# Attention of layer 1: the packed products of two steps in one visit to the array, where each step had its own

## The chip, the cores and the metric

One core of a Trainium2 chip runs the whole program. The metric is device time in microseconds (us). All data lie in the device's memory at the start and the results are written back there. The engines that matter here are TensorE (PE in the profile, with its weight loads as PEld), VectorE (DVE), ScalarE (ACT) and GpSimd (POOL); SyncE (SP) issues the DMAs.

## What is computed

The program has two layers on four images of 56x56 pixels and 256 channels. Layer 0 is a windowed attention. Layer 1 is full attention over the 3136 pixels of an image, and then an expert network. The change touches only the full attention of layer 1. Cut to what matters, its reference is:

```python
def _L1_attn_ref(x, w_qkv, b_qkv, w_out, b_out):
    qkv = x @ w_qkv + b_qkv                       # x: (4, 3136, 256), eight heads of 32
    q, k, v = jnp.split(qkv, 3, axis=-1)
    ...
    dots = jnp.einsum('bhid,bhjd->bhij', q, k) * scale
    attn = jax.nn.softmax(dots, axis=-1)
    out = jnp.einsum('bhij,bhjd->bhid', attn, v)
    ...
    return out @ w_out + b_out
```

The kernel subtracts from the dots of a query their exact maximum, takes the exponential, multiplies by V and by ones (the second gives the softmax's denominator), and divides at the end.

## The kernel before

`layer1_attend` works on eight *quads* (`QUADS = 2 * B`): four heads of one image each. A quad is 175 *steps* (`STEPS = NG * KT`): 7 groups `j` of 448 queries times 25 tiles `t` of 128 keys (the last tile of 64). The first quad and the last are written out, the six between are one loop body.

In step `n` TensorE makes four score products, one for each head (L1219, 98 rows by 128 columns of weights, 448 columns streamed), into three PSUM banks that rotate: product `i` waits until ScalarE has taken the exponential of product `i - 3` (L1348, output `a_P`). Between the scores stand the products that find the maxima for the *next* quad (L1150, the same shape, names `a_hk`, `a_hq`): 700 for a quad, spread by `maxima_by` over steps 4 to 167, so that a step has four or five. They too have three banks (`MAXES = 3`): product `i` waits until VectorE has reduced product `i - 3` to its row maximum (L1248, output `a_tops`). Steps 0 to 3 and 168 to 174, and the whole last quad, have none.

After the scores of a step comes a *burst*. Its parts are *packed*: four products with 32 columns of weights each, one for each head, side by side in the array, so that they run at the same time. There are three kinds:

- `mix` (L1170): one step's exponentials times V, into the bank MIX.
- `sum_pair` (L1186): the exponentials of two steps, added up by GpSimd (L1371, output `a_added`), times ones, into the bank SUM.
- for the last tile of a group, which has no partner, the exponentials times ones directly (L1175).

Which parts stand in the burst after step `n` is set by a small planner, `bursts()`. A mix is due after the scores of the next step, a sum three steps after its second step (`SUM_LAG = 3`). ScalarE's order follows from it: `TAKE_AT` and `TAKE_SUMS_AT` say before which step's exponentials ScalarE copies MIX and SUM out (L1318, L1323). The first mix of a group waits for that copy (`taken`).

VectorE goes through the steps in order: a step's maxima, and then, in the 7th to 11th step of a group, one of four reciprocals of the previous group's sums (`invert`, L1271, a quarter each) or the multiplication by them (`divide`, L1277). The exponentials lie in a ring of five steps (`RING = 5`), GpSimd's sums in a ring of three pairs.

Of the kernel before, what the change touches and what calls it, by code (L numbers as in the profile page):

```python
# [854 lines left out]
def layer1_attend(nc, A, S):  # L855
# [5 lines left out]
    with ExitStack() as ctx:  # L861
# [7 lines left out]
        STEPS = NG * KT  # L869
# [74 lines left out]
        def bursts():  # L944

            out, mixes, sums = [], [], []
            for n in range(2 * STEPS):
                j, t = divmod(n % STEPS, KT)
                mixes.append((n // STEPS, n % STEPS))
                if t % 2 == 1:  # L950
                    sums.append((n, (n // STEPS, j, t // 2)))
                parts = []
                if True:
                    while sums and sums[0][0] <= n - SUM_LAG:
                        parts.append(("sum",) + sums.pop(0)[1])
                    while mixes and mixes[0][0] * STEPS + mixes[0][1] < n:
                        parts.append(("mix",) + mixes.pop(0))
                out.append(parts)
            return out[:STEPS], out[STEPS:]

        opening, steady = bursts()
        tail = [part for parts in steady for part in parts if part[1] == 0]
        carried = [[(part[0], part[1] - 1) + part[2:] for part in parts] for parts in steady]
# [1193 lines left out]
```

## Time and profile before

| | us |
|---|---|
| median of 3 runs | 7947.33 (7942.66 to 7951.0) |
| the profiled execution, whole | 7931.02 |
| its span in the trace | 7929.2 |
| full attention of layer 1, from its first product to its last | 1789 to 6679 |
| thereof the first 700 maxima alone | 1789 to 2163 |

Over the span PE is busy 90%, DVE 68%, ACT 51% and POOL 47%. A matmul's busy time includes the time it takes to pass through the array, so neighbours overlap: what the engine spends on one is read from the distance between two starts, not from the durations. The same holds of VectorE's and ScalarE's instructions: a merged row of five says when the first started and when the last ended. Times in the text are from the span's start.

### The profile page before, as it was taken

To read this page: it belongs to the slowest core of one execution; us is meant where nothing else is said; L and a number is where in the kernel's file an instruction comes from. 1 tells how busy PE (TensorE), PEld (TensorE's weight loads), DVE (VectorE), ACT (ScalarE), POOL (GpSimd) and SP (SyncE) were. 2 spreads that over 40 slices of the span, in tenths; PEclk is the share of its full clock that TensorE was granted. 3 is DMA by queue.
4 is the path that set the end of the run, shared out by engine and by line. 5 is a ranking of instruction groups with operands and counts; after the bars stand their busy time and mean duration, and the time that the engine had idled before them with its cause. 6 is when DMAs were issued, how large, how long until landed. Compare 5 with 4: busy or idle time off the path is not lost. (4 is left out here: it accounts for less than half of the span.)

```text
span 7929.2 us, 152182 instructions
## 1 busy us (share of the span) xinstructions
PE 7120.8 (90%) x47408; PEld 4323.5 (55%) x47408; DVE 5376.1 (68%) x12877; ACT 4022.7 (51%) x9367; POOL 3714.0 (47%) x2395
## 2 busy tenths in 40 slices
PE   4459998989999999999999999999999888709999
PEld 2347776655455455455455455455455334608888
DVE  3359997659977677677677677677677102618888
ACT  0049997220055655565565555555565664104444
POOL 4011111110066666666666666666666665365554
PEclk8779999995599999999999999999999999859999
DMA  5442323871001201211211211211211102611221
GB/s 158 137 118 68 98 70 93 253 234 44 13 23 30 64 24 38 58 26 36 57 34 28 60 36 26 57 35 33 59 30 37 28 3 67 205 33 56 62 57 31
DMA packets 403136, 519.85 MB, mean 66 GB/s; under 512 B 64096, under 2 KB 355474, under 8 KB 399063
## 3 DMA queue, kind: packets, MB, share of 16 engines
q1 hardware_dynamic: 379687, 469.02, 21.9%
q0 software_dynamic: 22640, 40.75, 1.9%
q8 instruction: 421, 6.90, 0.4%
q14 instruction: 388, 3.18, 0.1%
HBM read 339.07 MB, written 200.10 MB: 68 GB/s over the span
## 5 line engine op out<-in xcount | busy, mean ns | idle before, releaser
L1248 DVE TENSOR_REDUCE a_tops<-a_ps 128x1 f32<-128x448 f32 (+1 forms) x5600 | 3071.8, 612 | 1092.9 <-PE a_ps L1150 1075.2
L1371 POOL TENSOR_TENSOR a_added<-a_P 128x896 f32<-128x896 f32 x1344 | 2799.3, 2102 | 2095.8 <-ACT a_P L1348 2095.8
L1348 ACT ACTIVATE a_P<-a_ps 128x448 f32<-128x448 f32 (+1 forms) x5600 | 2656.6, 547 | 2123.5 <-PE a_ps L1219 2081.9
L1219 PE MATMUL a_ps<-a_qp,a_kp 98*128 98x448 f32 (+1 forms) x5600 | 2154.1, 400 | 104.2 <-ACT a_P L1348 77.2
L1150 PE MATMUL a_ps<-a_hk,a_hq 96*128 96x448 f32 (+1 forms) x4900 | 1818.4, 381 | 2.0 <-DMA a_hq<-scratch_q 1.9
L1219 PEld LDWEIGHTS a_ps<-a_qp,a_kp 98*128 98x128 f32 (+1 forms) x5600 | 1028.9, 187 | 1296.0 <-ACT a_P L1348 741.0
L1170 PE MATMUL a_ps<-a_P,a_vt 128*32 128x448 f32 (+1 forms) x11200 | 1335.1, 549 | 0.0
L1150 PEld LDWEIGHTS a_ps<-a_hk,a_hq 96*128 96x128 f32 (+1 forms) x4900 | 916.4, 187 | 263.6 <-DVE a_tops L1248 170.3
L1186 PE MATMUL a_ps<-a_added,a_ones 128*32 128x448 f32 x5376 | 649.0, 555 | 0.0
L1170 PEld LDWEIGHTS a_ps<-a_P,a_vt 128*32 128x32 f32 (+1 forms) x11200 | 290.1, 109 | 513.9 <-issue 386.4
L550 ACT ACTIVATE n_P<-n_sm,n_mx 112x280 f32<-112x280 f32 x896 | 467.9, 522 | 108.4 <-DVE n_mx L498 108.3
L1271 DVE RECIPROCAL a_sums<-a_sums 128x112 f32<-128x112 f32 x224 | 185.0, 835 | 488.8 <-ACT a_sums L1323 488.8
L451 PE MATMUL n_ps<-n_idn,n_P 112*98 112x112 f32 x2688 | 421.2, 267 | 10.2 <-DVE n_P L508 10.2
L448 PE MATMUL n_ps<-n_idn 112*112 112x112 f32 x1792 | 373.1, 291 | 30.7 <-ACT n_PTs L557 29.8
L498 DVE CUSTOM_DVE_ANT_0 n_sm<-n_ps,n_bias 112x280 f32<-112x280 f32 x896 | 349.2, 445 | 72.3 <-PE n_ps L440 48.7
L557 ACT ACTIVATE n_PTs<-n_ps 98x336 f32<-98x336 f32 x896 | 391.1, 437 | 2.6 <-PE n_ps L451 2.0
L1138 PE MATMUL a_ps<-a_kp,a_qp 96*128 96x448 f32 (+1 forms) x700 | 370.2, 726 | 22.4 <-DMA a_kp<-scratch_k 22.4
L414 POOL CAST n_qp<-n_qn 128x784 fp32r<-128x784 f32 x32 | 52.5, 1639 | 673.7 <-DMA n_kn<-scratch_qk 338.2
L508 DVE TENSOR_SCALAR n_P<-n_P,n_rc 112x280 f32<-112x280 f32 x896 | 334.2, 415 | 16.0
L1951 ACT ACTIVATE e_h<-e_ps,e_b 128x512 f32<-128x512 f32 (+1 forms) x256 | 172.0, 672 | 336.2 <-PE e_ps L1911 311.8
L1924 PE MATMUL e_ps<-e_w2h,e_hTh 128*128 128x256 f32 (+1 forms) x1024 | 295.4, 289 | 37.0 <-DVE e_widest L2033 37.0
L448 PEld LDWEIGHTS n_ps<-n_idn 112*112 112x112 f32 x1792 | 255.4, 183 | 112.5 <-ACT n_PTs L557 98.9
(195 smaller groups left out, 7787.2 us busy)
## 6 DMA issues: line engine op xcount, KB each, us to landing
a_qp<-scratch_q SPq DMA_DIRECT2D x168, 224.0 KB, 3.9
a_kp<-scratch_k SPq DMA_DIRECT2D x96, 320.0 KB, 5.5
a_hk<-scratch_k SPq DMA_DIRECT2D x84, 336.0 KB, 5.0
scratch_t<-o_ts SPq DMA_DIRECT2D x56, 448.0 KB, 5.5
scratch_vw<-scratch_v SPq DMA_DIRECT2D x56, 392.0 KB
n_vt<-scratch_vw SPq DMA_DIRECT2D x64, 343.0 KB
a_hq<-scratch_q SPq DMA_DIRECT2D x84, 200.0 KB, 3.2
e_w<-in_w SPq DMA_DIRECT2D x16, 1024.0 KB, 7.1
```

The costliest lines, as they stand in the source:

```text
L448: pe.matmul(PS[0:TT, turn_bank(m), 384:384 + TT], idn[:, :], idn[:, :], start=True, stop=True)
L451: last = pe.transpose(PS[0:CHUNK, turn_bank(m), TT * c:TT * c + TT], P[:, m % RP, k0:k0 + CHUNK], idn[:, :])
L550: act.activation(P[:, m % RP, :], sm[:, m % 4, :], ACT.Exp, bias=mx[:, m % 8:m % 8 + 1], scale=-1.0, accum_out=rs[:, m % 8:m % 8 + 1]).the ...
L557: act.activation(PTs[:, m % 8, :], PS[0:CHUNK, turn_bank(m), 0:3 * TT], ACT.Copy).then_inc(copied, 1)
L1138: pe.matmul(PS[0:rows_of(t), i % FIRST_BANKS, 0:GW], qp[0:96, hh, 128 * t:128 * t + rows_of(t)], kp[0:96, hh, GW * k:GW * k + GW], start=T ...
L1150: pe.matmul(PS[0:rows_of(t), MAX + i % MAXES, 0:GW], hq[:, 128 * t:128 * t + rows_of(t)], hk[:, GW * k:GW * k + GW], start=True, stop=True ...
L1170: last = pe.matmul(PS[HD * hh:HD * hh + HD, MIX, 0:GW], vt[0:rows, t, HD * hh:HD * hh + HD], P[0:rows, (2 * n + hh // 2) % (2 * RING), hh ...
L1186: last = pe.matmul(PS[HD * hh:HD * hh + HD, SUM, 0:GW], ones[:, :], added2[:, (2 * (PAIRS * j + u) + hh // 2) % 6, hh % 2, :], start=(u == ...
L1219: pe.matmul(PS[0:rows_of(t), i_s % 3, 0:GW], kp[0:98, hh, 128 * t:128 * t + rows_of(t)], qp[0:98, hh, GW * j:GW * j + GW], start=True, sto ...
L1248: dve.tensor_reduce(tops[0:rows_of(t), KT * hh + t, k:k + 1], PS[0:rows_of(t), bank, 0:GW], AX_X, ALU.max).then_inc(topped, 1)
L1348: act.activation(P[0:rows_of(t), (2 * n + pair) % (2 * RING), hh % 2, :], PS[0:rows_of(t), (4 * n + hh) % 3, 0:GW], ACT.Exp).then_inc(expe ...
L1371: pool.tensor_tensor(added2[:, a % 6, :, :], P[:, (2 * n + pair) % (2 * RING), :, :], P[:, (2 * n + 2 + pair) % (2 * RING), :, :], ALU.add ...
```

## The change

One condition in the planner. Before, each step has its burst; now only the steps of odd number inside a quad have one, and it holds everything that is due by then: two mixes, and a sum for nearly every burst. A quad has 175 steps, so the last burst of a quad is after step 173, the next after step 1 of the following quad, and that one has the mixes of three steps. Sums whose third step is even come one step later than before. `maxima_by`, and so the order of VectorE's work, stays as it was.

```diff
                 if t % 2 == 1:
                     sums.append((n, (n // STEPS, j, t // 2)))
                 parts = []
-                if True:
+                if n % STEPS % 2 == 1:
                     while sums and sums[0][0] <= n - SUM_LAG:
                         parts.append(("sum",) + sums.pop(0)[1])
                     while mixes and mixes[0][0] * STEPS + mixes[0][1] < n:
                         parts.append(("mix",) + mixes.pop(0))
```

The order of TensorE's instructions in the first quad, in steps with maxima. L1219 are scores, L1150 are products for maxima, L1186 is a sum and L1170 a mix. Before:

```order
L1186 MATMUL a_ps<-a_added,a_ones 32x448 x4
L1170 MATMUL a_ps<-a_P,a_vt 32x448 x4
L1219 MATMUL a_ps<-a_qp,a_kp 128x448
L1150 MATMUL a_ps<-a_hk,a_hq 128x448
L1219 MATMUL a_ps<-a_qp,a_kp 128x448
L1150 MATMUL a_ps<-a_hk,a_hq 128x448
L1219 MATMUL a_ps<-a_qp,a_kp 128x448
L1150 MATMUL a_ps<-a_hk,a_hq 128x448
L1219 MATMUL a_ps<-a_qp,a_kp 128x448
L1150 MATMUL a_ps<-a_hk,a_hq 128x448
L1170 MATMUL a_ps<-a_P,a_vt 32x448 x4
```

The same engine and quad now, the end of a stretch of sixteen scores and maxima and the burst behind it:

```order
L1219 MATMUL a_ps<-a_qp,a_kp 128x448
L1150 MATMUL a_ps<-a_hk,a_hq 128x448
L1219 MATMUL a_ps<-a_qp,a_kp 128x448
L1150 MATMUL a_ps<-a_hk,a_hq 128x448
L1219 MATMUL a_ps<-a_qp,a_kp 128x448
L1150 MATMUL a_ps<-a_hk,a_hq 128x448
L1219 MATMUL a_ps<-a_qp,a_kp 128x448
L1150 MATMUL a_ps<-a_hk,a_hq 128x448
L1186 MATMUL a_ps<-a_added,a_ones 32x448 x4
L1170 MATMUL a_ps<-a_P,a_vt 32x448 x8
```

A visit to the array with one or two packed products came after four or five maxima; now one with three comes after eight or nine.

VectorE's order where the reciprocals stand, which is the same before and now. L1248 are maxima, L1271 reciprocals, L1277 the multiplication:

```order
L1248 TENSOR_REDUCE a_tops<-a_ps 128x1 x19
L1271 RECIPROCAL a_sums<-a_sums 128x112
L1248 TENSOR_REDUCE a_tops<-a_ps 128x1 x4
L1271 RECIPROCAL a_sums<-a_sums 128x112
L1248 TENSOR_REDUCE a_tops<-a_ps 128x1
L1248 TENSOR_REDUCE a_tops<-a_ps 64x1
L1248 TENSOR_REDUCE a_tops<-a_ps 128x1 x3
L1271 RECIPROCAL a_sums<-a_sums 128x112
L1248 TENSOR_REDUCE a_tops<-a_ps 128x1 x4
L1271 RECIPROCAL a_sums<-a_sums 128x112
L1248 TENSOR_REDUCE a_tops<-a_ps 128x1 x4
L1277 TENSOR_TENSOR a_yo<-a_y,a_sums 128x448
```

Nothing moved on VectorE; but of the steps whose maxima stand ahead of a reciprocal, those of even number have no burst behind them any more.

TensorE where a group of odd number ends (the second group of the first quad), now; L1175 is the last tile times ones. Before, the two L1170 stood in two bursts, with a step's scores between them:

```order
L1219 MATMUL a_ps<-a_qp,a_kp 128x448
L1150 MATMUL a_ps<-a_hk,a_hq 128x448
L1186 MATMUL a_ps<-a_added,a_ones 32x448 x4
L1170 MATMUL a_ps<-a_P,a_vt 32x448 x4
L1175 MATMUL a_ps<-a_P,a_ones 32x448 x4
L1170 MATMUL a_ps<-a_P,a_vt 32x448 x4
L1219 MATMUL a_ps<-a_qp,a_kp 128x448
```

The last mix of a group and the first of the next, which waits for the copy of the bank between them, now share a burst. The same piece before:

```order
L1170 MATMUL a_ps<-a_P,a_vt 32x448 x4
L1175 MATMUL a_ps<-a_P,a_ones 32x448 x4
L1219 MATMUL a_ps<-a_qp,a_kp 128x448
L1150 MATMUL a_ps<-a_hk,a_hq 128x448
L1219 MATMUL a_ps<-a_qp,a_kp 128x448
L1150 MATMUL a_ps<-a_hk,a_hq 128x448
L1219 MATMUL a_ps<-a_qp,a_kp 128x448
L1150 MATMUL a_ps<-a_hk,a_hq 128x448
L1219 MATMUL a_ps<-a_qp,a_kp 128x448
L1150 MATMUL a_ps<-a_hk,a_hq 128x448
L1186 MATMUL a_ps<-a_added,a_ones 32x448 x4
L1170 MATMUL a_ps<-a_P,a_vt 32x448 x4
```

## Rows read from the trace of the kernel before

**Rows 1.** Stretches: first maxima; quads with maxima; last quad; behind the attention.

```profile
core 0: us, PE busy (x) PEld busy (x) DVE busy (x) ACT busy (x) POOL busy (x), PEclk, DMA share, GB/s
1778.16:2162.90 384.74, 370.21 (x700) 198.34 (x700) 373.05 (x702) 0.00 (x0) 3.62 (x1) 0.50 0.12 26
2164.00:6162.00 3998.00, 3948.99 (x24597) 2071.81 (x24598) 2899.45 (x5175) 2375.43 (x4976) 2439.03 (x1171) 0.99 0.17 40
6162.00:6682.00 520.00, 460.81 (x2935) 171.88 (x2934) 30.18 (x41) 341.98 (x736) 360.31 (x174) 1.00 0.04 11
```

**Rows 2.** Timeline of PE, two steps with four maxima each, and their bursts.

```profile
start us, us, engine line op out<-in xcount [idle before <-releaser]
3003.44 0.96 PE L1170 MATMUL a_ps<-a_P,a_vt 128*32 128x448 f32 x8
3004.33 0.47 PE L1219 MATMUL a_ps<-a_qp,a_kp 98*128 98x448 f32 x1
3004.64 0.37 PE L1150 MATMUL a_ps<-a_hk,a_hq 96*128 96x448 f32 x1
3004.84 0.36 PE L1219 MATMUL a_ps<-a_qp,a_kp 98*128 98x448 f32 x1
...
3005.87 0.37 PE L1150 MATMUL a_ps<-a_hk,a_hq 96*128 96x448 f32 x1
3006.17 0.96 PE L1186 MATMUL a_ps<-a_added,a_ones 128*32 128x448 f32 x8
3006.95 0.94 PE L1170 MATMUL a_ps<-a_P,a_vt 128*32 128x448 f32 x8
3007.82 0.47 PE L1219 MATMUL a_ps<-a_qp,a_kp 98*128 98x448 f32 x1
```

**Rows 3.** Timeline of PE, the next step, with five maxima.

```profile
3008.96 0.37 PE L1219 MATMUL a_ps<-a_qp,a_kp 98*128 98x448 f32 x1
3009.22 0.48 PE L1150 MATMUL a_ps<-a_hk,a_hq 96*128 96x448 f32 x1
3009.53 0.36 PE L1219 MATMUL a_ps<-a_qp,a_kp 98*128 98x448 f32 x1
3009.75 0.47 PE L1150 MATMUL a_ps<-a_hk,a_hq 96*128 96x448 f32 x1
3010.14 0.58 PE L1170 MATMUL a_ps<-a_P,a_vt 128*32 128x448 f32 x4
```

**Rows 4.** Timeline of DVE over the same steps and the next.

```profile
3005.04 2.21 DVE L1248 TENSOR_REDUCE a_tops<-a_ps 128x1 f32<-128x448 f32 x4 [0.52 <-PE a_ps L1150]
3008.54 2.75 DVE L1248 TENSOR_REDUCE a_tops<-a_ps 128x1 f32<-128x448 f32 x5 [0.52 <-PE a_ps L1150]
3011.20 0.84 DVE L1271 RECIPROCAL a_sums<-a_sums 128x112 f32<-128x112 f32 x1
3011.97 2.15 DVE L1248 TENSOR_REDUCE a_tops<-a_ps 128x1 f32<-128x448 f32 x4
```

**Rows 5.** Waits of PEld (its own, and of DVE) from 3000 to 4000 us.

```profile
engine line waited for: us in total, times, longest us
PEld a_ps L1150 <- DVE a_tops L1248: 41.9, 164, 0.4
...
DVE a_tops L1248 <- PE a_ps L1150: 275.2, 257, 31.5
```

**Rows 6.** Line L1138, the first 700 maxima: its starts and waits.

```profile
L1138 PE MATMUL a_ps<-a_kp,a_qp x700: 575/734/742, 1788.9 to 2158.5; 96*128 96x448 f32 x168, 96*64 96x448 f32 x7
its engine sat idle before it (us, times) until:
  DVE a_tops L1248: 169.2, 683
```

**Rows 7.** Timeline of PE, the step in which the reciprocal of rows 4 delays VectorE.

```profile
3011.03 0.47 PE L1219 MATMUL a_ps<-a_qp,a_kp 98*128 98x448 f32 x1
...
3012.59 0.47 PE L1150 MATMUL a_ps<-a_hk,a_hq 96*128 96x448 f32 x1
3012.99 0.96 PE L1186 MATMUL a_ps<-a_added,a_ones 128*32 128x448 f32 x8
```

**Rows 8.** Timeline of all engines, one step of the last quad at a group's end.

```profile
6390.42 0.88 PE L1219 MATMUL a_ps<-a_qp,a_kp 98*128 98x448 f32 x3
6391.01 1.85 ACT L1348 ACTIVATE a_P<-a_ps 128x448 f32<-128x448 f32 x4 [1.35 <-PE a_ps L1219]
6391.61 0.47 PE L1219 MATMUL a_ps<-a_qp,a_kp 98*128 98x448 f32 x1 [0.31 <-ACT a_P L1348]
6392.00 0.96 PE L1170 MATMUL a_ps<-a_P,a_vt 64*32 64x448 f32 x8
6392.78 0.93 PE L1175 MATMUL a_ps<-a_P,a_ones 64*32 64x448 f32 x8
6393.03 0.54 ACT L1318 ACTIVATE a_y<-a_ps 128x448 f32<-128x448 f32 x1 [0.16 <-PE a_ps L1170]
```

**Rows 9.** GpSimd's sums from 3000 to 4000 us.

```profile
L1371 POOL TENSOR_TENSOR a_added<-a_P 128x896 f32<-128x896 f32 x293 | 610.6, 2103 | 389.4 <-ACT a_P L1348 389.4
```

**Rows 10.** Timeline of PE between two quads, at the lower clock: a burst of two.

```profile
4466.84 1.72 PE L1186 MATMUL a_ps<-a_added,a_ones 128*32 128x448 f32 x8
4468.33 1.72 PE L1170 MATMUL a_ps<-a_P,a_vt 128*32 128x448 f32 x8
4469.98 0.87 PE L1219 MATMUL a_ps<-a_qp,a_kp 98*128 98x448 f32 x3
```

## The prediction

> **What bounds the kernel now.** I first cut the span into stretches [rows 1]. The seven quads whose maxima are made beside them take from 2164 to 6162 us, 571 us each, with PE busy 98.8% of the time, DVE 73%, ACT 59%. A busy PE is not yet a bound, so I read its timeline next, by distances between starts. In a step with four maxima [rows 2] the second product starts 0.31 us behind the first (3004.33, 3004.64), the following ones 0.205 apart (3004.64 to 3005.87 are six distances), and the burst 0.30 behind the last (3006.17). Scores and maxima of such a step take 3004.33 to 3006.17, 1.84 us, without a wait. The burst of one mix takes 0.89 (3003.44 to 3004.33), that of sum and mix 1.65 (3006.17 to 3007.82); so a packed product more costs 0.76, and of the 0.89 some 0.14 is the way back to the full array.
>
> The step with five maxima looks different [rows 3]. By distances it would take 1.84 + 0.205 = 2.05; it takes 2.32 (3007.82 to 3010.14). Its last two maxima have a record of 0.48 and 0.47 us in place of 0.37: their weights were loaded late, after a wait. Rows 4 tell for what: VectorE's five reductions take 2.75 us, the last of them 0.61, so they follow each other every (2.75 - 0.61)/4 = 0.53 us, while TensorE offers a maximum every 0.41. With three banks product m+3 waits for reduction m. The view of waits counts 164 such waits in a thousand microseconds, only 42 us in all [rows 5], because four maxima are just what three banks and one reduction absorb, and then the burst gives VectorE time. The first 700 maxima, which have no bursts between them, show the limit naked [rows 6]: 369.6/700 = 0.528 us each, 683 of them waiting for VectorE. So the kernel is bound by TensorE, and VectorE stands right behind it, with the burst of every step as its time to catch up.
>
> **The change, part by part.** Two steps that stood apart now form one phase of eight scores, and behind it one burst of three packed products. Per pair of steps; a quad has 87.5 of them, all eight quads 700.
>
> *Bursts.* Before 0.89 + 1.65 = 2.54, now 1.65 + 0.75 = 2.40: 0.14 less, 700 times: -98 us.
>
> *Phases with maxima.* From the phase's start, the first maximum's product starts at 0.31, its reduction 0.40 later (3004.64 to 3005.04 [rows 2, 4]), at 0.71; reduction m ends at 0.71 + 0.61 + 0.53m. The product that waits for it is recorded 0.06 later (3008.54 + 0.61 = 3009.15 against 3009.22 [rows 3, 4]) and, its weights loaded late, streams another 0.11 later: 1.49 + 0.53m. The burst follows 0.29 behind. For five maxima the last waits for m = 1: 2.02 + 0.29 = 2.31, and the row has 2.32, so the recurrence holds. For eight, m = 4: 3.61 + 0.29 = 3.90, against 2 x 1.84 = 3.68 before, and 3.50 if nobody waited. For nine, 4.43, against 1.84 + 2.32 = 4.16. A quad has its 700 maxima on 82 pairs: 38 with eight and 44 with nine. 38 x 0.22 + 44 x 0.27 = 20.2 us, times seven quads: +141 us.
>
> *Reciprocals.* The one at 3011.20 holds the next reduction up for 0.77 (3011.97) [rows 4]. Before, a burst stands behind each, and hides most of it: the phase behind it takes 1.96 instead of 1.84 (3011.03 to 3012.99) [rows 7], and of the four in a group one or two show at all: some 0.15 us a group. Now two of the four stand between the maxima of an even step and of an odd one, inside a phase in which VectorE already sets the pace, and nothing hides them: 0.76 each. In the four groups of even number the multiplication stands there as well; its own place isn't in these rows, but with its 448 columns it is nearest to a reduction, 0.53. So 14 x 0.76 + 4 x 0.53 = 12.8 us in a quad, less 7 x 0.15 that they cost before: 11.7, times seven: +82 us. The ends are 0, if VectorE's slack takes them after all, and +90.
>
> *Phases without maxima.* They are 5.5 pairs in each of seven quads and 87.5 in the last, 126 in all. Here ScalarE sets the pace [rows 8]: exponentials every (1.85 - 0.54)/3 = 0.43 us, the fourth score waits for the first of them, and scores take 6390.42 to 6392.00 = 1.58. With eight scores four more come at 0.43: 3.30, against 3.16: +0.14, times 126: +18 us, and with the bursts these parts break even.
>
> *The copy of MIX.* At the end of the groups of odd number and at the quad's end, four times a quad, the first mix of a group now stands in the burst of the last mix of the group before, and waits for ScalarE's copy. In rows 8 the copy ends at 6393.57, 1.57 us after the mix began; mix and ones have passed by 1.52. With the latency of 0.06 and the late weights of 0.11 that is 0.2 us, 32 times: +6 us. Ends 0 and 1 us each, since a copy behind a full queue of exponentials could come later.
>
> *At no cost.* GpSimd needs 4.2 us for a pair and idles 39% [rows 9]; a sum that comes a step later still frees its buffer before GpSimd wants it (three pairs, six steps). The slot of exponentials that ScalarE overwrites in step n has its mix in the burst of n-3 at the latest, a step early; were this cover gone, each phase would wait a whole burst, 2.4 us. SyncE's loads of the next keys and values wait for mixes two steps or more before the burst in question, and its other waits are on scores. Between quads three steps of scores follow each other and one burst is long, at the lower clock in part: the same products in another order, 0 to 2 us a quad; I take 0.
>
> Sum: -98 + 141 + 82 + 18 + 6 = +149. The profiled execution took 7931, so 8080; the median of the runs lies 16 above it, so **8096 us**.
>
> **Rivals.** *A. The visits are what costs, and VectorE keeps up.* One visit less saves 0.10 at the way in, 0.10 at the first distance behind it and 0.14: 0.34 us. If no wait came for it (phase 3.50 and burst 2.40, against 3.68 and 2.54), 700 visits give -238 us, less 6: 7947 - 232 = 7715. The Trainium skill says, in "TensorEngine Tiling (Array Packing)", Key Properties, that changing the tiling mode drains the engine; by that rule alone half the drains go and this is the time. The rows agree that a change of mode costs [rows 2]. What speaks against A: the reductions would have to follow each other every 0.41 us, and in 700 in a row they took 0.528 [rows 6]. It decides on the third bank: from four maxima in a phase on TensorE waits. Chance 0.06. The same page warns, under PSUM Bottleneck, that tiling speeds up TensorE and not the emptying of PSUM, which may then bound; that is the forecast's side.
>
> *B. The reciprocals are hidden.* VectorE idles 275 us of a thousand now [rows 5]; if it got ahead during the long burst so that a reciprocal cost nothing, 82 us go: 8014. Against it: VectorE can't work ahead of the products, and the reciprocal stands in mid phase. With half of it, and the phases a little cheaper than worked out, the time is anywhere from 7965 to 8040. Chance 0.09.
>
> *C. The clock.* In the first 700 maxima, one product each 0.53 us, the granted clock was 0.50 for 370 us [rows 1, 6]. Now phases of the last quad have a score each 0.43 us for 3.3 us at a stretch. If that took the clock down, a packed product costs 1.49 instead of 0.76 [rows 10]: 2.2 us a pair, 88 pairs: +190 in the last quad, 8150 to 8290. Against it: the phases with maxima have two products each 0.53, and a full burst stands between phases everywhere. Chance 0.06.
>
> *D. Nothing to be measured:* the order shows that the bursts did move, so only gains and losses that happen to cancel would do it, as when VectorE gains on the phases what the visits don't save. Chance 0.02.
>
> **How the numbers follow.** The forecast has 0.77. Its terms' ends are 8014 (reciprocals hidden) and some 8135 (reciprocals at 90, boundaries at 2 us a quad, copies at 1 us). The range 8040 to 8135 holds the forecast's case and little of the others, about 0.8. A measurement tells some 0.2% (16 us) from no change. Faster by more than that is A, 0.06, and 0.01 for what I don't see; within it D and the low end of B, 0.03; slower 0.90.
>
> **What would show it.** In the changed kernel's timeline a phase of eight maxima takes 3.90 and one of nine 4.43, with maxima from the fifth on recorded at 0.47 and 0.53 apart; the burst of three takes 2.40. PEld's waits of L1150 for L1248 rise from 42 us in a thousand to 150 or more. Phases with a reciprocal in the middle take 0.76 more. A quad takes about 590 us in place of 571. The last quad stays within 3 us. Phases of 3.5 us would make A right, and phases with a reciprocal no longer than others B; a granted clock below 0.95 in the last quad C.

## The result: 2.1% slower

| | us | ratio to before |
|---|---|---|
| kernel before, median of 4 runs | 7944.99 (7941.22 to 7951.0) | |
| changed kernel, median of 4 runs | 8114.07 (8104.34 to 8118.08) | 1.021 (1.0193 to 1.0228) |
| predicted | 8096 (8040 to 8135) | |

The change costs 169 us; the forecast was 149. The profiled execution of the changed kernel took 8113.66 (span 8111.9), 183 more than the profiled one before, but 12 of these lie behind the attention, where nothing was changed: from the last score to the end it is 1254.5 us before and 1266.4 after, and among all kernels shown below, which have the same work there, it lies anywhere from 1254 to 1276. So the attention is where to look; its own difference is 171 us.

The stretches of the changed kernel, to be held against [rows 1] (quads with maxima, last quad):

```profile
core 0: us, PE busy (x) PEld busy (x) DVE busy (x) ACT busy (x) POOL busy (x), PEclk, DMA share, GB/s
2164.00:6308.00 4144.00, 4029.73 (x24595) 2029.25 (x24596) 2847.63 (x5172) 2410.42 (x4976) 2437.33 (x1172) 0.99 0.16 39
6308.00:6853.00 545.00, 512.20 (x2941) 191.21 (x2937) 32.58 (x42) 332.73 (x736) 359.97 (x173) 0.96 0.04 10
```

The seven quads with maxima take 4144 us against 3998, and the last 545 against 520 (what of the latter lies behind the last product is the same in both). The last quad's row also shows something new in the PEclk column: 0.96, where before it had 1.00.

One phase of eight maxima without a reciprocal, and the burst before it, in TensorE's timeline (answers to [rows 2, 3]):

```profile
3394.11 1.69 PE L1170 MATMUL a_ps<-a_P,a_vt 128*32 128x448 f32 x16
3395.73 0.47 PE L1219 MATMUL a_ps<-a_qp,a_kp 98*128 98x448 f32 x1
3396.04 0.37 PE L1150 MATMUL a_ps<-a_hk,a_hq 96*128 96x448 f32 x1
...
3397.70 0.43 PE L1150 MATMUL a_ps<-a_hk,a_hq 96*128 96x448 f32 x1
...
3398.72 0.47 PE L1150 MATMUL a_ps<-a_hk,a_hq 96*128 96x448 f32 x1
...
3399.25 0.47 PE L1150 MATMUL a_ps<-a_hk,a_hq 96*128 96x448 f32 x1
3399.66 0.58 PE L1186 MATMUL a_ps<-a_added,a_ones 128*32 128x448 f32 x4
```

The phase takes 3395.73 to 3399.66, 3.93 us. The first four maxima are 0.41 apart; from the fifth on (3397.70) they are recorded at 0.43 to 0.47 instead of 0.37, with late weights, and 0.53 apart (3398.72, 3399.25): VectorE's pace. Its own timeline at the same place and in two phases before it, and then the two engines' rows in the view of waits from 3000 to 4000 us (answers to [rows 4, 5]):

```profile
3382.09 2.21 DVE L1248 TENSOR_REDUCE a_tops<-a_ps 128x1 f32<-128x448 f32 x4 [1.22 <-PE a_ps L1150]
3384.23 0.84 DVE L1271 RECIPROCAL a_sums<-a_sums 128x112 f32<-128x112 f32 x1
3384.99 2.14 DVE L1248 TENSOR_REDUCE a_tops<-a_ps 128x1 f32<-128x448 f32 x4
...
3391.19 0.62 DVE L1277 TENSOR_TENSOR a_yo<-a_y,a_sums 128x448 f32<-128x448 f32 x1
3391.72 2.74 DVE L1248 TENSOR_REDUCE a_tops<-a_ps 128x1 f32<-128x448 f32 x5
3396.45 4.34 DVE L1248 TENSOR_REDUCE a_tops<-a_ps 128x1 f32<-128x448 f32 x8 [1.98 <-PE a_ps L1150]
```

```profile
PEld a_ps L1150 <- DVE a_tops L1248: 172.3, 642, 0.9
...
DVE a_tops L1248 <- PE a_ps L1150: 311.8, 136, 31.7
```

The last eight reductions run without a break, 4.34 us. At 3384.23 a reciprocal stands in the middle of a phase, and the next reduction starts 0.76 later; at 3391.19 the multiplication does, 0.53. TensorE's weights for maxima now wait for VectorE 642 times in a thousand microseconds, before 164 times; and at the same time VectorE waits for TensorE longer than before (312 against 275), because it stands idle during the long burst (1.98 us ahead of the last row). Both wait for each other more than they did, as two engines do when their work comes in larger lumps and the banks between them are few; no run gave the maxima more banks.

The account of the attention, from the starts of scores and bursts in both traces:

| part | before | after | difference | forecast |
|---|---|---|---|---|
| steps 4 to 167 of seven quads | 3743.4 | 3895.0 | +151.6 | +147 |
| from step 168 to step 4 of the next quad, seven times | 259.3 | 258.4 | -0.9 | +1 |
| last quad, steps 4 to 174 | 486.6 | 507.1 | +20.5 | +1 |

The forecast column is the prediction's terms put to these places. In the first row these are 141 + 82 for the phases, 82 x 7 x 0.14 = 80 off for the bursts, and three copies a quad. In the other two the longer phases and the shorter bursts cancel and only copies are left.

### The profile page after: what moved, and what is told of

Same layout as the page of the kernel before. It is cut to its first block and busy times, and to the rows that moved or that the text cites. A ratio compares the mean times of both kernels' runs of the same rounds, so it can differ in the third digit from the quotient of the medians.

```text
span 8111.9 us, 152188 instructions
## 1 busy us (share of the span) xinstructions
PE 7259.4 (89%) x47408; PEld 4306.5 (53%) x47408; DVE 5327.8 (66%) x12877; ACT 4049.4 (50%) x9367; POOL 3710.3 (46%) x2395
## 5 line engine op out<-in xcount | busy, mean ns | idle before, releaser
L1248 DVE TENSOR_REDUCE a_tops<-a_ps 128x1 f32<-128x448 f32 (+1 forms) x5600 | 3031.1, 613 | 1280.3 <-PE a_ps L1150 1263.0
L1219 PE MATMUL a_ps<-a_qp,a_kp 98*128 98x448 f32 (+1 forms) x5600 | 2141.0, 394 | 71.6 <-ACT a_P L1348 37.8
L1150 PE MATMUL a_ps<-a_hk,a_hq 96*128 96x448 f32 (+1 forms) x4900 | 2039.8, 421 | 74.3 <-DVE a_tops L1248 64.3
L1219 PEld LDWEIGHTS a_ps<-a_qp,a_kp 98*128 98x128 f32 (+1 forms) x5600 | 1041.7, 188 | 790.9 <-issue 525.9
L1150 PEld LDWEIGHTS a_ps<-a_hk,a_hq 96*128 96x128 f32 (+1 forms) x4900 | 909.5, 186 | 775.1 <-DVE a_tops L1248 713.1
L1170 PE MATMUL a_ps<-a_P,a_vt 128*32 128x448 f32 (+1 forms) x11200 | 1206.1, 545 | 0.0
L1170 PEld LDWEIGHTS a_ps<-a_P,a_vt 128*32 128x32 f32 (+1 forms) x11200 | 355.5, 111 | 716.5 <-issue 554.4
L1186 PE MATMUL a_ps<-a_added,a_ones 128*32 128x448 f32 x5376 | 657.1, 562 | 0.0
L1271 DVE RECIPROCAL a_sums<-a_sums 128x112 f32<-128x112 f32 x224 | 185.1, 835 | 511.0 <-ACT a_sums L1323 511.0
L1138 PE MATMUL a_ps<-a_kp,a_qp 96*128 96x448 f32 (+1 forms) x700 | 370.2, 726 | 22.3 <-DMA a_kp<-scratch_k 22.3
```

Of the source, the lines that this page charges most:

```text
L1150: pe.matmul(PS[0:rows_of(t), MAX + i % MAXES, 0:GW], hq[:, 128 * t:128 * t + rows_of(t)], hk[:, GW * k:GW * k + GW], start=True, stop=True ...
L1170: last = pe.matmul(PS[HD * hh:HD * hh + HD, MIX, 0:GW], vt[0:rows, t, HD * hh:HD * hh + HD], P[0:rows, (2 * n + hh // 2) % (2 * RING), hh ...
L1186: last = pe.matmul(PS[HD * hh:HD * hh + HD, SUM, 0:GW], ones[:, :], added2[:, (2 * (PAIRS * j + u) + hh // 2) % 6, hh % 2, :], start=(u == ...
L1219: pe.matmul(PS[0:rows_of(t), i_s % 3, 0:GW], kp[0:98, hh, 128 * t:128 * t + rows_of(t)], qp[0:98, hh, GW * j:GW * j + GW], start=True, sto ...
L1248: dve.tensor_reduce(tops[0:rows_of(t), KT * hh + t, k:k + 1], PS[0:rows_of(t), bank, 0:GW], AX_X, ALU.max).then_inc(topped, 1)
```

## The experiments

Each time is a median, and the ratio behind it is to runs of the kernel before on the same chip. For half_b, half_a, recip_a and ahead_b the kernel before took 7946.03. The other four ran on another chip, where it took 7936.13, so their times stand some 10 us low beside the rest.

### half_b and half_a: VectorE's part of the phases taken away

The same edit in the kernel before (half_b) and in the changed one (half_a). It leaves out half the columns of each maximum from the second quad on, so VectorE's reductions become shorter and TensorE's work stays:

```diff
-                dve.tensor_reduce(tops[...], PS[0:rows_of(t), bank, 0:GW],
+                dve.tensor_reduce(tops[...], PS[0:rows_of(t), bank, 0:width],
...
-                        maximum(m, i, (i // HMX, i % KT, i // KT % NG), MAX + i % MAXES)
+                        maximum(m, i, (i // HMX, i % KT, i // KT % NG), MAX + i % MAXES, GW // 2)
```

> The kernel before, with the maxima of the second to the eighth quad taken over 224 of their 448 columns (so half of that work is left out and the result of those quads rests on other maxima). Theory (VectorE with three banks paces the phases): only the 308 steps with five maxima waited, 0.27 us each, so about 83 us less than before: 7860. Rival (the product itself, not VectorE, takes longer in those steps): 7945.

> The changed kernel with the same half of the maxima's columns left out. Theory: no wait for VectorE is left in a phase, so a pair costs one visit less and nothing else, 0.34 us: 574 pairs with maxima give 195 us less than half_b, the last quad's 20 us stay: about 7690. Rival (the long burst of three packed products costs by itself, or ScalarE paces the phases): half_a no faster than half_b, 7860 or more.

Measured: half_b 7862.74 (ratio to before 0.9895, 0.988 to 0.991), half_a 7729.47 (0.9727, 0.9712 to 0.9741). A phase of nine in half_a, with the reductions from VectorE's timeline under it:

```profile
3307.89 0.47 PE L1219 MATMUL a_ps<-a_qp,a_kp 98*128 98x448 f32 x1
3308.20 0.57 PE L1150 MATMUL a_ps<-a_hk,a_hq 96*128 96x448 f32 x2
...
3311.29 0.37 PE L1150 MATMUL a_ps<-a_hk,a_hq 96*128 96x448 f32 x1
3311.59 0.96 PE L1186 MATMUL a_ps<-a_added,a_ones 128*32 128x448 f32 x8
```

```profile
3308.61 3.47 DVE L1248 TENSOR_REDUCE a_tops<-a_ps 128x1 f32<-128x224 f32 x9 [2.61 <-PE a_ps L1150]
```

With reductions of 0.39 us the phase takes 3.70 us in place of 4.45 (its median in the changed kernel), a phase of eight 3.50 in place of 3.92. With the burst that is 5.89 for a pair of steps in half_a against 6.24 in half_b (1.85 + 1.85 + 0.89 + 1.64, the medians of its phases and bursts): one visit to the array saves 0.34 us, as the prediction's rival A had priced it. So the change does save what it is built to save. With VectorE's limit eased it is a gain of 133 us, 1.7% (half_b against half_a); with the limit, it is a loss of 169. A gain of 170 was expected (7860 to 7690). Steps 4 to 167 gained 147.1, not 195: 574 x 0.342 = 196, of which some 39 are still lost within the phases (their mean lies above their median by 0.05 and 0.08 us; the excess lies in the phases with a reciprocal or a multiplication in the middle), and the groups' ends, below, take some 9. The last quad lost 15.5 and the quads' boundaries 6.

### recip_a: the reciprocals where a burst follows

```diff
-                        if 6 <= n % KT < 10:
-                            invert(q if j >= 0 else q - 1, j % NG, n % KT - 6)
-                        if n % KT == 10:
+                        late = n % KT - 6
+                        if n % 2 == 1 and 0 <= late < 8:
+                            invert(q if j >= 0 else q - 1, j % NG, late // 2)
+                        if n % 2 == 1 and 8 <= late < 10:
                             divide(q if j >= 0 else q - 1, j % NG)
```

> The changed kernel with VectorE's reciprocals and the multiplication all behind the maxima of odd steps, where a burst follows. Theory: the 0.76 us that each of two per group cost in mid phase, and the multiplication in four groups, are hidden again: 75 to 80 us less than the changed kernel's 8114: about 8037. Rival (they were hidden already and the phases' excess has another cause): 8114.

Measured: 8029.99 (1.0104, 1.0088 to 1.0119), 84 us less than the changed kernel; steps 4 to 167 went from 3895.0 to 3810.3. Phases of nine now have a mean of 4.449 beside a median of 4.452, where the changed kernel has 4.613 and 4.455. The reciprocals and multiplications in mid phase are half of the change's loss.

### ahead_b and ahead_recip_a: VectorE's chain started earlier

In ahead_b, made from the kernel before (in ahead_recip_a, made from recip_a, the condition is `n % 2 == 0 and due > i`):

```diff
                     due = maxima_by(n + 1) if more else 0
+                    ahead = more and due - i == 5
                     for hh in range(4):
+                        if ahead and hh == 0:
+                            product_for_maximum(m, i)
+                            i += 1
                         i_s = 4 * n + hh
```

> The kernel before, with one change of order on TensorE: in a step with five maxima the first maximum's product stands ahead of the first score instead of behind it. Theory: VectorE's chain of reductions starts a product and the late weights earlier, 0.2 us, and ends so much earlier, so such a step takes 2.11 in place of 2.32: 308 times, 62 us less than before: 7883. Rival (TensorE's own work or ScalarE, whose first score comes 0.2 us later, sets the step): 7945 or slower.

> The changed kernel with the reciprocals behind odd steps, as in recip_a, and the first maximum's product of every phase ahead of the first score. Theory: both halves of VectorE's pace are then taken off as far as three banks allow: recip_a's 8030 less 0.20 us in each of 574 phases: 7915. Rival (in long phases the order within the phase does not matter): 8030.

Measured: ahead_b 7886.39 (0.9924, 0.991 to 0.9937), ahead_recip_a 7910.59 (0.9966, 0.9954 to 0.9978). A step with five maxima in ahead_b, whose scores are L1223:

```profile
3024.99 0.47 PE L1150 MATMUL a_ps<-a_hk,a_hq 96*128 96x448 f32 x1
3025.30 0.37 PE L1223 MATMUL a_ps<-a_qp,a_kp 98*128 98x448 f32 x1
...
3026.76 0.43 PE L1150 MATMUL a_ps<-a_hk,a_hq 96*128 96x448 f32 x1
3027.12 0.96 PE L1186 MATMUL a_ps<-a_added,a_ones 128*32 128x448 f32 x8
```

It takes 2.13 us, against 2.32 in [rows 3]: the last maximum's product waits 0.06 instead of 0.27. In ahead_recip_a phases of nine went from 4.45 to 4.25 us and phases of eight from 3.92 to 3.72 (medians), 0.21 less where 0.20 was expected. So the recurrence that the prediction rests on holds in short phases and in long ones, and both times came within 5 us of the expected 7883 and 7915. ahead_b is faster than the kernel before, and with both of VectorE's burdens eased even the changed order is, by 0.3%; but it isn't faster than ahead_b.

### fill_a: what the last quad lost

In the changed kernel's last quad no maxima are made, and phases and bursts were expected to break even, but it lost 20.5 us. The granted clock shows where. Two stretches next to each other in the changed kernel's last quad:

```profile
6550.00:6554.40 4.40, 3.96 (x24) 1.61 (x20) 0.00 (x0) 3.69 (x9) 2.29 (x2) 1.00 0.02 6
6554.40:6557.80 3.40, 3.40 (x24) 0.75 (x16) 1.88 (x3) 0.95 (x2) 1.85 (x1) 0.50 0.00 0
```

and TensorE's timeline there:

```profile
6553.96 1.33 PE L1186 MATMUL a_ps<-a_added,a_ones 128*32 128x448 f32 x8
6555.05 3.07 PE L1170 MATMUL a_ps<-a_P,a_vt 128*32 128x448 f32 x16
6558.04 0.88 PE L1219 MATMUL a_ps<-a_qp,a_kp 98*128 98x448 f32 x3
```

The clock fell from 1.00 to 0.50, from 2.4 to 1.2 GHz, for 3.4 us, just behind a phase of eight scores, and the burst took 4.08 us (6553.96 to 6558.04) instead of 2.39. There are ten such stretches between the last quad's fifth step and its end, and each begins within 0.5 us of the end of a phase of eight. (The expectation below says eleven. The further one lies ahead of the fifth step, at the boundary of the quads, and lasts 6.8 us; the kernel before has such falls, of 10.2 us, at five of its seven boundaries, but not at this one.) In the last quad before there is none. Ten stretches of 3.4 us at half speed are 17 us of lost work.

The other runs agree. The three kernels that also have phases of eight scores with three banks show the same falls of 3.4 us in the last quad: half_a seven, recip_a and ahead_recip_a ten each. half_b and ahead_b, which keep single bursts, show none.

```diff
                         until = i + (due - i + 3 - hh) // (4 - hh)
+                        if not more and (n % 2 == 0 and hh == 3 or n % 2 == 1 and hh < 3):
+                            pe.matmul(PS[0:rows_of(t), MAX + hh % MAXES, 0:GW],
+                                      kp[0:98, hh, 128 * t:128 * t + rows_of(t)],
+                                      qp[0:98, hh, GW * j:GW * j + GW], start=True, stop=True)
```

> The changed kernel; in the last quad, behind the fourth to the seventh score of each phase of eight, the score's product is made once more into a bank that nobody reads. The gaps of 0.22 us in which TensorE waits for ScalarE there take it. The trace of the changed kernel shows the last quad 20.5 us longer than before (507.1 against 486.6 from its fifth step to its last) and eleven stretches of 3.4 us with the granted clock at 0.5 in it. Theory (these falls of the clock are the 20 us, and they come because TensorE does so little in such a phase): with the gaps filled the falls go, last quad 487 to 490, whole 8095. Rival (the 20 us are waits at the groups' ends or for ScalarE): last quad 507 or longer.

Measured: 8090.26 (1.0194, 1.0179 to 1.021), with 349 more products in it. By the ratios (the changed kernel has 1.021, 1.0193 to 1.0228) that is some 13 us less than the changed kernel, and the two intervals overlap, so the whole time alone would not show it. The trace does: the last quad takes 490.0 us instead of 507.1, and the granted clock is 1.00 all through it. One phase, with the scores L1219 and the added products L1223:

```profile
6502.38 0.87 PE L1219 MATMUL a_ps<-a_qp,a_kp 98*128 98x448 f32 x3
6503.56 0.47 PE L1219 MATMUL a_ps<-a_qp,a_kp 98*128 98x448 f32 x1 [0.31 <-ACT a_P L1352]
6503.88 0.37 PE L1223 MATMUL a_ps<-a_qp,a_kp 98*128 98x448 f32 x1
...
6505.39 0.40 PE L1219 MATMUL a_ps<-a_qp,a_kp 98*128 98x448 f32 x1
6505.71 0.96 PE L1186 MATMUL a_ps<-a_added,a_ones 128*32 128x448 f32 x8
```

It is as long as without them, 3.33 us, so the added work lay wholly in gaps, and what it changed was the clock. So the falls are 17 of the 20.5 us, and products in the gaps prevent them. The other 3.4 us stay when the falls are gone; in half_a, whose seven falls take 12 of its 15.5 us, about as much stays.

### six_ahead_b and six_a: no bank to wait for

In the last quad the three banks of the maxima stand empty. Both kernels give them to the scores there; six_ahead_b is made from ahead_b, six_a from the changed kernel:

```diff
-                        if i_s >= 3:
-                            pe.wait_ge(exped, q * HS + i_s - 2)
+                        banks = 3 if more else 6
+                        if i_s >= banks:
+                            pe.wait_ge(exped, q * HS + i_s - banks + 1)
...
-                        pe.matmul(PS[0:rows_of(t), i_s % 3, 0:GW],
+                        pe.matmul(PS[0:rows_of(t), i_s % banks, 0:GW],
...
-                                       PS[0:rows_of(t), (4 * n + hh) % 3, 0:GW], ACT.Exp).then_inc(exped, 1)
+                                       PS[0:rows_of(t), (4 * n + hh) % (3 if more else 6), 0:GW], ACT.Exp).then_inc(exped, 1)
```

> ahead_b, and in the last quad, which makes no maxima, the scores rotate through six banks instead of three. Theory: its phases no longer wait for ScalarE, 1.03 in place of 1.58 us, 175 times: 97 us less than ahead_b's 7886: 7790, last quad 390. Rival (ScalarE, or GpSimd with 4.2 us for each pair of steps, sets the last quad's pace anyway): 7840 or more.

> The changed kernel with six banks for the scores of the last quad. Theory: with no bank to wait for, the visit that the change saves is a gain: a phase of eight takes 1.84 in place of 3.33 us, a pair 4.24 against 4.60 with single bursts; last quad 360 against the 390 of six_ahead_b, whole about 7967. The granted clock stays at 1.00 there. Rival (the visits' saving is lost to GpSimd's 4.2 us a pair or to ScalarE): last quad no shorter than six_ahead_b's.

Measured: six_ahead_b 7776.15 (0.9794, 0.9781 to 0.9808), the fastest of all, 160 us under the kernel before; six_a 7974.23 (1.0051, 1.0036 to 1.0067). Last quads: 388.3 and 379.4 us, against 486.6 and 507.1 with three banks. Two steps in six_ahead_b, and two in six_a, with the scores as L1224 and L1220:

```profile
6201.48 1.07 PE L1224 MATMUL a_ps<-a_qp,a_kp 98*128 98x448 f32 x4
6202.48 0.96 PE L1170 MATMUL a_ps<-a_P,a_vt 128*32 128x448 f32 x8
6203.37 1.09 PE L1224 MATMUL a_ps<-a_qp,a_kp 98*128 98x448 f32 x4
6204.38 0.96 PE L1186 MATMUL a_ps<-a_added,a_ones 128*32 128x448 f32 x8
6205.16 0.94 PE L1170 MATMUL a_ps<-a_P,a_vt 128*32 128x448 f32 x8
6206.02 1.07 PE L1224 MATMUL a_ps<-a_qp,a_kp 98*128 98x448 f32 x4
```

```profile
6403.78 2.09 PE L1220 MATMUL a_ps<-a_qp,a_kp 98*128 98x448 f32 x8
6405.80 0.96 PE L1186 MATMUL a_ps<-a_added,a_ones 128*32 128x448 f32 x8
6406.57 1.69 PE L1170 MATMUL a_ps<-a_P,a_vt 128*32 128x448 f32 x16
6408.19 1.07 PE L1220 MATMUL a_ps<-a_qp,a_kp 98*128 98x448 f32 x4
```

A pair takes 4.54 us with single visits and 4.41 with one: here the changed order wins, by 0.13 and not by the 0.36 expected for it. The phase of eight takes 2.02 instead of 1.84: even with six banks its last scores wait, since ScalarE stands idle in the bursts (0.8 us ahead of each eight exponentials) and then needs 0.43 us for each exponential, while scores come every 0.2 us. So six_a's last quad came 19 us above the 360 expected, and its granted clock stayed at 1.00.

## Why the prediction was right, and where it was off

The time lay in the range and 18 us above the point, by these steps:

- **What bounds the kernel:** right. TensorE, with VectorE right behind it, which the bursts of each step kept off the path. half_b shows that only the steps of five maxima waited (83 us expected, 83 measured; steps of four take 1.85 us in both).
- **Bursts:** 0.89 + 1.65 became 2.39, as worked out.
- **Phases with maxima:** 3.92 and 4.45 us in the median where the recurrence gave 3.90 and 4.43: +147 for the +141. half_a, with faster reductions, turned the loss into a gain, and the two kernels with a maximum ahead moved it by as much as the recurrence says.
- **Reciprocals:** right. The forecast has 89 us for those in mid phase, less 7 that they cost before: +82. Phases with a reciprocal in the middle are 0.67 to 0.70 us above the median of their kind, not 0.76, and those with the multiplication 0.52 (0.53 was taken): 81 us. Taking them out of the middle gave back 84, to be held against the 89. Rival B, by which they would have cost nothing, is thereby excluded.
- **Phases without maxima:** the step that failed. Their length was right (3.33 for 3.30), but the prediction let bursts and phases break even and said that the last quad would stay within 3 us. Without the falls of the clock it nearly does (3.4 us in fill_a). It named the clock as rival C and put its price at 190 us, as if the clock stayed down throughout, with a chance of 0.06. What came is a small part of it, ten falls of 3.4 us, most of 20.5 us. A cause that acts for part of the time should have stood in the range of the forecast, not only as an all-or-nothing rival.
- **The copy of MIX:** a term was missing beside it. The term was 6 us for 32 copies; the bursts at the 48 ends of groups inside the quads cost some 10 us more than the bursts' term says. In all 48 the burst now goes over from 128 rows of weights to the last tile's 64, which takes 0.11 us: 5 us that the prediction has nowhere, and half of them at groups of even number, where no copy is waited for. At the 24 groups of odd number the next mix then starts 0.86 us (18 times) or 0.93 us (6 times) behind the ones, where 0.78 is usual. How much of that is the wait for the copy and how much the way back to 128 rows was not measured, so the 0.2 us of the prediction is neither confirmed nor refuted as a wait.
- **At no cost:** right as far as the traces show. GpSimd idles 414 us of a thousand, and ScalarE waits for it twice in a thousand, 6.5 us together. The time between the quads is the same.
- **The sum:** the attention took 171 us more where 149 were forecast, and errors partly cancel in that. The last quad (some 20 us), the phases with maxima (6) and the ends of groups (4) came on top, while the reciprocals were 5 to 8 us cheaper. That the last quad alone is as large as the whole miss of 18 us is in part chance.
- **Rival A:** its price of a visit, 0.34 us, was right, and its condition was not met. The Trainium skill says in "TensorEngine Tiling (Array Packing)", Key Properties, that a change of tiling mode drains TensorE. The trace agrees that a change costs: half_a gains 0.34 us with each visit less, though no run shows that the cost is a drain. On the same page, under PSUM Bottleneck, the Trainium skill warns that emptying PSUM may become the bottleneck; the trace agrees, with 642 waits of maxima for VectorE in a thousand microseconds, and that is what decided.

## What to carry to other kernels

Merging visits to save switches makes lumps, and lumps need banks (shown for the scores of the last quad, argued for the maxima): before such a change, work out for each engine that empties the banks how long it runs alone on what they hold, and how long it then stands. Small jobs of that engine that a burst had hidden (here the reciprocals) must move to where a burst still follows; they were half of this loss. And look for banks that stand empty in a part of the program: three of them shortened the last quad by 98 us (486.6 to 388.3), more than any order of the products gave.

## What the runs showed of the hardware

The clock may fall although TensorE never stands still for long: in the records of the changed kernel's last quad, from its fifth step on, its pauses are mostly 0.31 us and 0.60 at most. There it makes eight products of 448 columns in 3.33 us, then a full burst of 2.39 us, and the granted clock fell to 0.50 ten times; with four products more in each phase it never fell, and neither did it in the kernel before, with four products in 1.58 us and bursts of 0.89 and 1.64 us. The busy share does not tell the two apart: PE is busy 512 of 545 us in the changed kernel and 461 of 520 in the one before [rows 1].

A change from weights of 128 rows to weights of 64 inside a burst of packed products costs 0.11 us. The burst at the end of a group of odd number:

```profile
6476.28 0.96 PE L1186 MATMUL a_ps<-a_added,a_ones 128*32 128x448 f32 x8
6477.17 0.96 PE L1170 MATMUL a_ps<-a_P,a_vt 64*32 64x448 f32 x8
6477.95 0.93 PE L1175 MATMUL a_ps<-a_P,a_ones 64*32 64x448 f32 x8
6478.88 0.96 PE L1170 MATMUL a_ps<-a_P,a_vt 128*32 128x448 f32 x8
```

From the first to the second are 0.89 us, where a burst without the change has 0.78 (3006.17 to 3006.95 [rows 2]; 6477.17 to 6477.95 here). At the groups of even number the change stands between two mixes and costs the same (0.865 instead of 0.752, medians). From the third to the fourth are 0.93, which holds the way back to 128 rows and the wait for ScalarE's copy; what each of these two has of it wasn't measured apart.
